# Graph attention on one core: all exchange transfers of the steady state issued by SyncE, with stores and row reloads in another order

## The reference

```python
h = jnp.maximum(_layernorm(x, axis=-1), 0.0)
q = h @ Wq.T + bq;  k = h @ Wk.T + bk;  v = h @ Wv.T + bv
a = q @ k.T / sqrt(256) + adj + adj
x = x + softmax(a, axis=-1) @ v
```

## Time and profile before

| | us |
|---|---|
| median of 3 runs | 712.77 |
| the three runs | 718.14, 712.77, 710.68 |
| profiled execution, its own time | 712.38 |
| profiled execution, span of the instructions | 710.6 |
| PE busy | 689.6 (97%) |
| DVE, ACT, POOL busy | 581.3, 431.6, 427.6 |

### The profile page before, as it was taken

One profiled execution on the slowest core, in us unless ns is written; L12 is line 12 of the kernel. 1 busy time (PEld: TensorE's weight loads), 2 busy tenths in 40 slices (PEclk: granted clock), 3 DMA queues, 4 the chain that ended last, 5 costly groups with the idle time before them and its releaser, 6 DMA issues.

```text
span 710.6 us, 14184 instructions
## 1 busy us (share of the span) xinstructions
PE 689.6 (97%) x4799; PEld 475.1 (67%) x4799; DVE 581.3 (82%) x1284; ACT 431.6 (61%) x732; POOL 427.6 (60%) x434
## 2 busy tenths in 40 slices
PE   5789999999999999999999999999999999999998
PEld 4556546676666666766766676667666667666786
DVE  4899788888888888788888888797877878887897
ACT  4899564756755675657576565746566665656440
POOL 1879506564754665665657474656637575655587
PEclk9999999999999999999999999999999999999999
DMA  8558699999999999999989898989998899988572
GB/s 267 172 161 263 169 249 302 267 234 245 216 225 240 242 250 203 261 224 266 232 239 236 215 249 237 249 229 234 211 253 222 243 230 228 249 234 211 127 208 68
DMA packets 85048, 160.99 MB, mean 227 GB/s; under 512 B 12784, under 2 KB 33648, under 8 KB 84976
## 3 DMA queue, kind: packets, MB, share of 16 engines
q1 hardware_dynamic: 64336, 126.39, 69.7%
q10 hardware_dynamic: 20640, 33.70, 20.1%
HBM read 80.35 MB, written 8.39 MB: 125 GB/s over the span
## 4 chain that ended last, share of the span: by engine, by line
PE 74%; DMA 13%; ACT 3%; SPq 3%; DVE 2%; issue 2%; POOL 1%; ACTq 1%; DVEq 0%; POOLq 0%
PE bank L1457 42%; PE bank L1524 32%; DMA xT<-rows 4%; DMA out_y<-xy 3%; DMA rows<-in_adj 3%; ACT rows L723 1%; DMA xy<-in_x 1%; PE bank L1471 1%; DMA rows<-in_x 1%; DMA g_scratch<-xT 1%; SPq L436 1%; SPq L426 1%; SPq L407 1%; ACTq L801 1%; DMA v_sb<-rows 1%
## 5 line engine op out<-in xcount | busy, mean ns | idle before, releaser
L641 POOL TENSOR_TENSOR wT<-xT,wT 128x512 f16<-128x512 f32 x233 | 267.4, 1163 | 191.0 <-ACT wT L818 190.9
L1457 PE MATMUL bank<-v_sb,wT 128*128 128x256 f16 x2796 | 342.6, 273 | 0.0
L1524 PE MATMUL bank<-top,a_op 128*128 128x512 f16 x1344 | 331.1, 379 | 3.3 <-DVE rows L1089 1.4
L1457 PEld LDWEIGHTS bank<-v_sb,wT 128*128 128x128 f16 x2796 | 273.6, 98 | 80.5
L818 ACT CAST wT<-xT 128x512 f16<-128x512 f32 x233 | 139.1, 611 | 141.8 <-DVE rows L1138 129.3
L1524 PEld LDWEIGHTS bank<-top,a_op 128*128 128x128 f16 x1344 | 130.8, 98 | 112.7 <-DVE rows L1096 3.1
L1111 DVE CUSTOM_DVE_ANT_0 rows<-bank,rows 128x512 f32<-128x512 f32 x256 | 173.7, 680 | 12.1 <-PE bank L1524 3.4
L792 ACT ACTIVATE rows<-rows,exp_bias,exp_scale 128x1024 f32<-128x1024 f32 x128 | 158.3, 1237 | 35.8 <-DVE exp_bias L1178 29.1
L1138 DVE STREAM_TRANSPOSE rows<-rows 128x1024 f32<-128x1024 f32 x128 | 158.4, 1239 | 0.2 <-ACT rows L792 0.2
L1096 DVE SCALAR_TENSOR_TENSOR rows<-rows,adj_scale,bank 128x512 f32<-128x512 f32 x64 | 47.8, 746 | 53.5 <-PE bank L1524 53.5
L1089 DVE SCALAR_TENSOR_TENSOR rows<-rows,adj_scale,bank 128x512 f32<-128x512 f32 x64 | 47.6, 744 | 27.8 <-PE bank L1524 20.9
(11 more groups left out here) (115 smaller groups left out, 452.7 us busy)
## 6 DMA issues: line engine op xcount, KB each, us to landing
rows<-in_adj SPq DMA_DIRECT2D x128, 512.0 KB, 8.1
xT<-rows SPq DMA_DIRECT2D x244, 128.0 KB, 4.2
xT<-rows ACTq DMA_DIRECT2D x244, 128.0 KB, 6.5
rows<-in_x SPq DMA_DIRECT2D x8, 512.0 KB, 6.0
xy<-in_x SPq DMA_DIRECT2D x32, 128.0 KB, 4.8
g_scratch<-xT SPq DMA_DIRECT2D x16, 256.0 KB, 4.6
g_pair<-g_scratch SPq DMA_DIRECT2D x15, 256.0 KB, 5.0
out_y<-xy SPq DMA_DIRECT2D x30, 128.0 KB, 7.9
```

The lines of the kernel that those rows point to most:

```text
L641: nc.gpsimd.tensor_tensor(split_piece(m, 1), exchanged(m), split_piece(m, 0), ALU.subtract).then_inc(split_lo, 1)
L1457: return nc.tensor.matmul(out_ap, stationary, moving, start=first, stop=last)
L1524: last = nc.tensor.matmul(ps[:], s, mv, start=first and k == 0, stop=k == 2, skip_group_check=True)
```

## The change

Three edits, all in the orders of SP and ACT; no transfer and no arithmetic is added or removed.

First, `exchange_b(u)` of units 0 to 59 is issued by SP in one go, right after its own wait for `turned`; ACT keeps the last four units. Second, in the steady state SP's iteration n has the order: both stores at its head (each when it is due), `exchange_a(u)`, `refill(u - 1, 1)`, `load_xy`, `load_g`, `exchange_b(u)`, `refill(u, 0)`. Third, the opening is put in a like order: `exchange_b(0)` stands between `store_g(4)` and `refill(0, 0)`, `move_v(6)` and `move_v(7)` stand ahead of `store_g(5)` and `store_g(6)`.

```diff
+            def exchange_b(u):
+                sp.wait_ge(turned, 2 * u + 2)
+                arrival_free(sp, u)
+                for i in range(P // Q):
+                    sp.dma_start(arrivals(u)[2 * Q:P, i].rearrange("p j q -> p (j q)"),
+                                 unit_row(u, 1)[i * Q:(i + 1) * Q, :]).then_inc(landing(u, 1), 16)
...
             exchange_a(0)
             store_g(4)
+            exchange_b(0)
             refill(0, 0)
+            move_v(6)
             store_g(5)
-            move_v(6)
             move_v(7)
+            store_g(6)
             sp.wait_ge(v_moved[0], 64 * (GROUPS // 2))
             load_rows(14)
-            store_g(6)
             store_g(7)
             refill(0, 1)
             exchange_a(1)
+            exchange_b(1)
             exchange_a(2)
             refill(1, 0)
+            exchange_b(2)
             refill(1, 1)
+            refill(2, 0)
 
             def period(n):
                 p, u = n // QUADS, n - EXP_LAG
                 if n % QUADS == 0 and p >= 3:
                     store(2 * (p - 3) + 1)
+                if n % QUADS == 3 and p >= 2:
+                    store(2 * (p - 2))
                 if unit_in_range(u):
                     exchange_a(u)
+                if unit_in_range(u - 1):
+                    refill(u - 1, 1)
                 if n % QUADS in (0, 1) and 2 <= p < PAIRS:
                     load_xy(2 * p + n % QUADS)
                 if n % QUADS == 0 and p + 1 < PAIRS:
                     load_g(p + 1)
-                if unit_in_range(u - 1):
-                    refill(u - 1, 0)
-                if unit_in_range(u - 1):
-                    refill(u - 1, 1)
-                if n % QUADS == 3 and p >= 2:
-                    store(2 * (p - 2))
+                if unit_in_range(u) and n < PERIODS:
+                    exchange_b(u)
+                if unit_in_range(u):
+                    refill(u, 0)
...
             def period(n):
                 p, u = n // QUADS, n - EXP_LAG
                 m = 4 * (n - WEIGH_LAG)
+                if n % QUADS:
+                    exponential(u, 0)
+                high(m + 2)
+                high(m + 3)
                 if n % QUADS == 0:
-                    exchange_b(u - 1, 0)
-                    high(m + 2)
-                    exchange_b(u - 1, 1)
-                    high(m + 3)
                     exponential(u, 0)
-                    exchange_b(u - 1, 2)
-                else:
-                    exponential(u, 0)
-                    exchange_b(u - 1, 0)
-                    high(m + 2)
-                    exchange_b(u - 1, 1)
-                    high(m + 3)
-                    exchange_b(u - 1, 2)
                 scale_adj(n)
-                exchange_b(u - 1, 3)
                 exponential(u, 1)
```

More of the change, by code:

```diff
@@ L948, in _ @@
             high_query(2)
-            exchange_b(0, 0)
             evict_g(4, 1)
             evict_g(5, 0)
-            exchange_b(0, 1)
             high_v(13)
@@ L958, in _ @@
             evict_g(5, 1)
-            exchange_b(0, 2)
             exponential(2, 0)
@@ L962, in _ @@
             evict_g(6, 0)
-            exchange_b(0, 3)
             exponential(2, 1)
@@ L970, in _ @@
             high(1)
-            exchange_b(1, 0)
             scale_adj(6)
-            exchange_b(1, 1)
-            exchange_b(1, 2)
-            exchange_b(1, 3)
             def period(n):
```

## The result

The changed kernel took 757.35 us (median of 4 runs, 751.88 to 765.92) against 712.88 for the kernel before (4 runs): a ratio of 1.059, 95% interval 1.049 to 1.068. The forecast was 711.2, the range 709.8 to 715.5. Nothing was computed or moved in other amounts (160.98 MB of DMA after, 160.99 before), and the time rose by 44 us.

What follows compares the result with a forecast made beforehand. It took DMA as the near bound, with PE's idle time leaving 1.9 us to win. From the profiled 712.38 us it took 1.42 for two stalls, other terms 0, giving 710.96; forecast 711.2, range 709.8 to 715.5.

Steps and rivals of the forecast that it cites:

- Row reloads: SP's row loads of adj: issued sooner, part 0 by 7 us, they remove two PE stalls, a gain of 1.42 us.
- One queue in place of two: Nearly all DMA on SP's queue: a lone queue carries as much, 232 against 234 GB/s, so cost 0.
- rival B: One queue carries less, 223 GB/s, so DMA sets a 10.26 us period: 722 to 739 us; chance 0.08.
- DMA is the near bound: Steady state: DMA share 1.05 at 234 GB/s, later 0.91 at 239, with some 2.29 MB in each 9.77 us period.
- Issue time: SP takes over 240 issues from ACT, 2.4 us a period, hidden by SP's slack of 3.5 us a period.
- Second half of the exchange: Issued by SP instead of ACT: costs nothing, with 8 us cover up to the cast and some 11 to PE.
- Stores at the head: Stores first in SP's iteration, load_xy behind a row load: between -4 and +2.2 us on ACT, nothing on PE.
- The opening: Reordered first part: store_g(5) at most 4.8 us later; bounds -0.3 and +2 us, taken as 0.
- The ceiling on the gain: PE's idle time in the steady state: an edit there can win 1.9 us at most, 0.3% of the time.
- What should be seen if B held: Sign in the profile after: PE gaps at each period, DMA share at its ceiling and less GB/s.

Runs made afterwards that it cites:

- e11: Only the kernel's transfers, no attention computed: a unit took 9.3 and 8.8 us grouped, 10.6 and 11.0 alternating, 8.6 and 8.5 on two queues.
- e13: Only transfers, all on SP's queue, 16 units a stretch: grouped 155.45 us, pieces of both halves in turn 125.09, halves alone plus rows alone 137.4.
- e1: Kernel before with SP's new order alone, ACT still issuing all second halves (two queues): 726.78 us, ratio 1.017.
- e3: Changed kernel with the row load of part 1 moved behind the second half of the exchange: 717.03 us, ratio 1.004.
- e9: Changed kernel, order untouched, loading only 768 of 1024 columns of each row from row 22 on: 716.39 us, ratio 0.998.
- e8: Changed kernel with the row load of part 1 behind the second half and the small loads ahead of the first half: 714.66 us, ratio 0.999.
- e12: e8 with the opening grouped too, both row loads of unit 1 behind both its halves and ahead of unit 2's: 711.72 us, ratio 0.996.
- e10: Kernel before, two queues, with the even store and the small loads moved to the head of the period: 715.97 us, ratio 1.001.
- e6: Changed kernel with only the row load of part 1 taken one unit older, at the same place: 779.17 us, ratio 1.090.
- e4: Changed kernel with the small loads (load_xy, load_g) ahead of the first half of the exchange: 769.84 us, ratio 1.069.
- e5: Changed kernel with both row loads of a period taken one unit older, at the same places: 759.75 us, ratio 1.063.
- e7: Changed kernel with only the row load of part 0 taken one unit older: 755.14 us (749.46 and 760.82), no ratio.
- e2: Kernel before with SP issuing the second half behind both row loads, opening as in the change: three runs at 738 us, one at 724.53.

## Why the prediction was wrong

The step that failed is *Row reloads*. It took moving `refill(u - 1, 1)` between the halves for a pure gain of 1.42 us, since it had only its waits and its cover in view, and it had no term for what the new order does to the rate of DMA. That term stood at nothing without a reason. With the second halves on SP too the queue went to half, row, half, row. By e11 this takes 10.8 us a unit where 9.77 are there (10.7 by e13), by e1 the order costs some 12 us even on two queues, by e3 one step of it is worth all but 3 of the 44 us, and by e9 the loss goes when there are fewer bytes to carry. Of the gain nothing is seen: one add of DVE waited 5.87 us for a row at 125 us, and PE 4.0 us behind it.

*One queue in place of two* is where the rate was priced, with "a lone queue carries as much for the same mix: cost 0". For one queue as such this came out right: e8 and e12 lose nothing on it. But the figure couldn't cover the change. It was a mean of 14 stretches in which SP's queue kept the engines full, and that queue held a half to two rows, in that order, where the changed one holds two halves to two rows in another order. The mean of 232 GB/s was also lifted by two stretches with 345 and 378; the median of the 14 is 210, under the 234 that were needed. That one queue still does as well is therefore partly luck.

The rival B had nearly the right size (a rate of 223 GB/s, 10.26 us a period, 739 us) and the wrong reason: one queue carries 242 GB/s in e3. It named 57 periods at 0.49 us; measured were 218 GB/s and 0.7 us. Its chance of 0.08 rested on the share of 1.05, which e11 shows to be no measure of capacity, and on SP's issue time, which holds halves by themselves to 198 GB/s in e13 but didn't keep the queue of e3 from 242. The prediction read the same share as "DMA is the near bound" and then gave no cost to two edits of DMA's queues.

The Trainium skill, in "DMA: Bandwidth & Descriptors", section "Issuing engines are not separate DMA queues", says that DMAs of all issuers run on the same 16 engines and that several issuers save only issue time. By that rule one queue costs nothing beyond issue time. e11 agrees to within 6%, with two queues ahead, and the e3 and e12 runs show a kernel on one queue that loses nothing or next to nothing. The loss lay in the order, on which I had let that rule reassure me.

Point by point, the rest:
- *Issue time* was right: SP issues L444 at a median of 0.599 us, and q10 has only 1440 packets left. SP was not full of issues; what it stood for were landings, 189.6 us, which the sum of 6.3 of 9.77 us leaves out.
- *Second half of the exchange*: the cover of 8 us up to the cast is not what gave way. The median landing is 6.0 us, and ACT's wait for `turned` ahead of its casts is gone, as foreseen.
- *Stores at the head*: the bound of +2.2 us on ACT for each xy was too small. It was 165.2 us in 28 waits, 5.9 each, against 41.9 in 17, since two things came together: an x tile takes 7.2 us to land in the median, 4.8 before, and it is issued later, behind SP's wait for a landing ahead of the row load, which the bound left out. "Nothing on PE" was wrong as a consequence: the wait goes on over ACT and POOL in their fixed orders. By e10 these moves bring no gain in the order of before.
- *The opening*: PE between 0 and 106 us is as before; the row loads between halves after that cost some 4 us up to 142 us, and e12 wins that part back by order alone.
- The ceiling on the gain (1.9 us by PE's idle time, 0.3%) isn't contradicted: the best version, e12, is ahead by 0.4%, with an interval from 0.0 to 0.8%, and its profiled execution, 712.76 us, is not ahead of that of before, 712.38.
- What should be seen if B held (PE's gaps, share at its ceiling, less GB/s) was seen, though the gaps came in many periods and not in each. The price of the gaps has a second part that the prediction had nowhere: 13.8 us more of PE's busy time, most of it from the lower clock behind the idle stretches, on top of 29.2 us more of idle time.

Open: which meeting in the DMA engines makes alternating dear, and why the same grouped stretch took between 140.76 and 155.45 us in e11 and e13; why e6, with one of the two row loads older, is slower than with both; whether the small loads at the head make e4 slower than the changed kernel (they do no harm in e8); how much of the loss of e5 and e7 is the lateness of row loads by itself; and why e2, whose queue has halves and rows in pairs, carries 220 GB/s: pairs are the better order in e3, e8, e11, e12 and e13, but by e2 they are not enough by themselves.

## What to carry to other kernels

A DMA queue near its limit has an order as well as a length: before a transfer is moved, write down what will stand before and behind it, and take the rate for that sequence from a stretch that has it, or measure the sequence alone, as e11 does in one run. A DMA share of 1 is no rate and no reserve; read the GB/s beside it, and multiply by the bytes of a period. When a chain runs round through landings and issues, it doesn't say whether the waits or the rate is the bound. Take out the waits (e5), some of the bytes (e9), or everything but the transfers (e11); each of the first two moves something else too, so it takes more than one.

## What the runs showed of the hardware

- In one queue, 128 KB SBUF-to-SBUF pieces in fours, alternating with 512 KB row loads, ran at 191, 195 and 198 GB/s (e11, e13); the same transfers as two fours and two rows at 216 to 239; with the pieces of the two halves in turn at 268 (e13, one stretch).
- Row loads alone ran at 309 GB/s on one queue, pieces alone at 198 with SP's issue time as the limit (128 KB in 0.66 us) (e13).
- The same work on two queues took 137.93 and 135.63 us where one grouped queue took 149.36 and 140.76 (e11), and 155.45 in e13.
- Six matmuls of 128x512 took 2.67 us at a granted clock of 0.55, just after PE had stood idle for 2.83 us, and 1.47 us at 1.00 (the kernels after and before).
